# Two-column operations of three norms on GpSimd, and a second variance taken as ScalarE's sum of squares of a Hadamard product

## The reference, cut to what matters

```python
def norm(x):  # over the last axis, eps = 1e-5
    m, v = mean(x), var(x)
    return (x - m) / sqrt(v + eps)

x = x + norm(attention(norm(x), Wq, bq, Wk, bk, Wv, bv, Wo, bo))
xh = norm(x) @ H                     # Hadamard / sqrt(512)
scale = max(max|xh| over the row, 1e-5) / 7
xq = clip(round(xh / scale), -8, 7) * scale
wq = ternary(weight) * scale_w       # one scale for each output row
x = x + norm(xq @ wq.T)
```

## Time and profile before

| | |
|---|---|
| median of three runs | 1216.96 us |
| profiled execution, its own time | 1213.31 us |
| its span | 1211.4 us |
| busy: PE, DVE, ACT, POOL | 91%, 83%, 58%, 49% |

### The profile page before, as it was taken

The page is one execution under the profiler, slowest core; times in us unless marked ns, Lnnn a source line. Parts: engine busy times, 40 slices in busy tenths (PEclk is TensorE's granted clock), DMA queues, the critical chain, the costliest instruction groups (busy, mean ns, idle before and its releaser), DMA issues.

```text
span 1211.4 us, 44874 instructions
## 1 busy us (share of the span) xinstructions
PE 1100.2 (91%) x18625; PEld 726.4 (60%) x18656; DVE 1009.3 (83%) x2558; ACT 702.7 (58%) x1494; POOL 599.1 (49%) x719
## 2 busy tenths in 40 slices
PE   5899999999999999999999999999999999999641
PEld 3566556666666666666566666666666666666320
DVE  5749998888988888899888888988888899887772
ACT  5454566666566566655666665566566655665431
POOL 2333545555454556555545555454556555445422
PEclk9999999999999999999999999999999999999875
DMA  9746665666666576566675656656575566654230
GB/s 271 165 110 138 124 130 136 159 138 136 134 125 137 142 146 153 125 136 138 122 145 137 159 134 137 136 125 132 142 149 145 131 137 138 124 129 102 72 70 36
DMA packets 204687, 161.81 MB, mean 134 GB/s; under 512 B 150432, under 2 KB 150688, under 8 KB 204384
## 3 DMA queue, kind: packets, MB, share of 16 engines
q1 hardware_dynamic: 199600, 141.34, 55.2%
q0 software_dynamic: 4880, 17.57, 4.1%
HBM read 40.87 MB, written 16.78 MB: 48 GB/s over the span
## 4 chain that ended last, share of the span: by engine, by line
PE 56%; DVE 32%; issue 7%; ACT 2%; SPq 1%; DMA 1%; POOL 1%; POOLq 0%; DVEq 0%; ACTq 0%
PE f_job L1281 42%; DVE f_bst L980 6%; PE f_st L1382 3%; DVE f_z L1058 3%; PE f_o L1399 2%; PE f_o L1404 2%; DVE f_o L970 2%; DVE f_inverse L972 2%; PE f_job L1426 2%; DVE f_rmax L948 2%; DVE f_x L1004 2%; DVE f_folded_x L1021 2%; DVE f_y L1012 2%; DVE f_y L1011 2%; DVE f_small L1006 1%
## 5 line engine op out<-in xcount | busy, mean ns | idle before, releaser
L469 POOL TENSOR_SCALAR_AFFINE_SELECT f_PT<-f_PT 64x512 f32<-64x512 f32 (+1 forms) x256 | 202.0, 810 | 68.6 <-ACT f_PT L635 42.8
L484 POOL TENSOR_TENSOR f_square<-f_stage 128x512 bf16<-128x512 f16 x128 | 130.8, 1044 | 130.7 <-ACT f_stage L613 117.5
L1281 PE MATMUL f_job<-f_xTh,f_wqh 128*128 128x256 f16 x512 | 140.8, 275 | 15.6 <-DVE f_wkl L809 14.4
L613 ACT ACTIVATE f_stage<-f_job,f_bias 128x256 f16<-128x256 f32 x256 | 106.0, 465 | 83.7 <-PE f_job L1281 76.9
L475 POOL TENSOR_TENSOR f_OTl<-f_o,f_OTh 128x256 f16<-128x256 f32 x128 | 86.3, 674 | 114.4 <-ACT f_OTh L653 113.6
L1281 PE MATMUL f_job<-f_xTl,f_wqh 128*128 128x256 f16 x512 | 140.2, 274 | 0.0
L1281 PE MATMUL f_job<-f_xTh,f_wql 128*128 128x256 f16 x512 | 140.2, 274 | 0.0
L1281 PE MATMUL f_job<-f_xTh,f_wkh 128*128 128x256 f16 x512 | 139.9, 273 | 0.0
L1281 PE MATMUL f_job<-f_xTh,f_wkl 128*128 128x256 f16 x512 | 139.8, 273 | 0.0
L1281 PE MATMUL f_job<-f_xTl,f_wkh 128*128 128x256 f16 x512 | 139.7, 273 | 0.0
L934 DVE SCALAR_TENSOR_TENSOR f_stage<-f_job,f_bias,f_stage 128x256 f16<-128x256 f32 x256 | 110.7, 474 | 29.5 <-ACT f_stage L613 27.5
(11 more groups left out here) (181 smaller groups left out, 3026.5 us busy)
## 6 DMA issues: line engine op xcount, KB each, us to landing
f_stacks<-f_stage SPq DMA_DIRECT2D x380, 128.0 KB
f_xin<-x SPq DMA_DIRECT2D x32, 512.0 KB, 4.6
f_x<-x SPq DMA_DIRECT2D x32, 512.0 KB, 4.0
out<-f_z POOLq DMA_DIRECT2D x32, 512.0 KB, 3.3
f_Vmix<-f_V SPq DMA_DIRECT2D x32, 256.0 KB, 3.2
f_Vmix<-f_V SPq DMA_DIRECT2D x64, 128.0 KB, 3.4
f_stacks<-rows_const SPq DMA_DIRECT2D x3, 512.0 KB, 7.8
f_stacks<-wqT SPq DMA_DIRECT2D x2, 512.0 KB, 6.0
```

The source lines that it names most:

```text
L469: nc.gpsimd.affine_select(out=d, in_=d, compare_op=ALU.is_ge, fill=0.0, base=odd * SUB, pattern=[[0, 4], [0, TP], [1, SUB]], channel_multi ...
L484: nc.gpsimd.tensor_tensor(square[:, 2 * m + pair, :], h, h, ALU.mult).then_inc(squared, 1)
L613: nc.scalar.activation(stage[:, 2 * m, g, :], bank("qk", g)[:, m * W2:(m + 1) * W2], ACT.Identity, bias=bias[:, m, g:g + 1]).then_inc(qk_h ...
L1281: mm = pe.matmul(dst, lhs[a](c), rhs[b](c), start=(n == 0), stop=(n == 3 * KC - 1))
```

## The change

What it does:

- f, y and z: variance + eps, the negated mean, the products that make the offsets, and z's difference of offsets go from VectorE to GpSimd, next to the powers that were there (`front_columns`, `y_columns`, `z_columns` in the places of the three roots). VectorE only makes `bn_stats` and `bn_aggr`.
- The x norm's statistics go away. ScalarE's new `square_sum` takes the sum of squares of columns 1 to 511 of the Hadamard product (Square with an accumulated output), before `round_levels` of each tile; GpSimd's `z_columns` makes eps from it.
- Column 0 of the quantized levels is a zero that is written once (`q16` gets memory of its own, set to zero at the start); largest magnitude, squares, rounding and levels work on 511 columns.
- ScalarE's order: `square_sum(k-1, 0)` and `round_levels(k-1, 0)` ahead of `front_norm(m, 0)`; `front_norm(m, 1)` behind the first two `exps`.
- The checks of ranges at the end use the new columns, and have one reduction and one addition more.

The diff, cut to its core:

```diff
-        q16 = x2h[:].bitcast(BF16)
+        q16 = sb("q16", [P, TP, D], BF16)
+        unread = sb("unread", [P, TP, D], BF16)
...
+            nc.gpsimd.memset(q16[:], 0.0).then_inc(pool_consts, 1)
+            pool.wait_ge(pool_consts, 7)
...
+            def y_columns(k):
+
+                pool.wait_ge(y_stats_made, TP * k + TP)
+                until(pool, x1_made, TP * k)
+                nc.gpsimd.tensor_scalar(y_veps, y_mv[:, :, 1], EPS, None, ALU.add).then_inc(y_veps_made, 1)
+                nc.gpsimd.tensor_scalar(y_off[:, k, :], y_mv[:, :, 0], -1.0, None, ALU.mult).then_inc(y_turned_sign, 1)
                 pool.wait_ge(y_veps_made, k + 1)
                 nc.gpsimd.tensor_tensor(y_rstd, y_veps, minus_half[:], ALU.pow).then_inc(y_rstd_made, 1)
...
+                pool.wait_ge(y_turned_sign, k + 1)
+                pool.wait_ge(y_rstd_made, k + 1)
+                nc.gpsimd.tensor_tensor(y_off[:, k, :], y_off[:, k, :], y_rstd, ALU.mult).then_inc(y_off_made, 1)
+
+            def z_columns(k):
+
+                pool.wait_ge(qinv_made, TP * k + TP)
+                pool.wait_ge(x_squared, TP * k + TP)
+                nc.gpsimd.tensor_scalar(qeps, x_ss[:, k, :], EPS * (SX * D) ** 2, EPS / D, ALU.add,
+                                        ALU.mult).then_inc(z_step, 1)
+                nc.gpsimd.tensor_tensor(qsquare, qinv, qinv, ALU.mult).then_inc(qsquare_made, 1)
+                pool.wait_ge(z_step, 4 * k + 1)
+                pool.wait_ge(qsquare_made, k + 1)
+                nc.gpsimd.tensor_tensor(qeps, qeps, qsquare, ALU.mult).then_inc(qeps_made, 1)
+                pool.wait_ge(qeps_made, k + 1)
+                pool.wait_ge(z_stats_made, TP * k + TP)
+                nc.gpsimd.tensor_tensor(z_veps, z_mv[:, :, 1], qeps, ALU.add).then_inc(z_step, 1)
+                pool.wait_ge(z_step, 4 * k + 2)
+                until(pool, z_normed, TP * k)
+                nc.gpsimd.tensor_tensor(z_mul, z_veps, minus_half[:], ALU.pow).then_inc(z_step, 1)
+                pool.wait_ge(z_step, 4 * k + 3)
+                nc.gpsimd.tensor_tensor(z_off, z_mv[:, :, 0], z_mul, ALU.mult).then_inc(z_step, 1)
+                pool.wait_ge(z_step, 4 * k + 4)
+                pool.wait_ge(y_off_made, k + 1)
+                nc.gpsimd.tensor_tensor(z_off, y_off[:, k, :], z_off, ALU.subtract).then_inc(z_cols, 1)
...
+            def square_sum(k, t):
+
+                act.wait_ge(qinv_made, TP * k + t + 1)
+                nc.scalar.activation(unread[:, t, 1:D], bank("h", t)[:, 1:D], ACT.Square,
+                                     accum_out=x_ss[:, k, t:t + 1]).then_inc(x_squared, 1)
...
                 qk_high_part(n, 2)
+                if has(k - 1):
+                    square_sum(k - 1, 0)
+                    round_levels(k - 1, 0)
                 if has(m):
                     front_norm(m, 0)
-                if has(k - 1):
-                    round_levels(k - 1, 0)
-                if has(m):
-                    front_norm(m, 1)
...
                 if has(m):
+                    front_norm(m, 1)
                     front_high(m)
                 exps(s, 1, 0)
                 exps(s, 1, 1)
                 if has(k - 1):
+                    square_sum(k - 1, 1)
                     round_levels(k - 1, 1)
...
             def y_stats(k):
                 dve.wait_ge(y_made, TP * k + TP)
-                statistics(0, y, y_mv)
-                nc.vector.tensor_scalar(y_veps, y_mv[:, :, 1], EPS, None, ALU.add).then_inc(y_veps_made, 1)
+                statistics(0, y)
+                until(dve, y_off_made, k)
+                for t in range(TP):
+                    nc.vector.bn_aggr(y_mv[:, t, :], bst[:, 0, t, :]).then_inc(y_stats_made, 1)
...
-                note(nc.vector.scalar_tensor_tensor(y_off[k % 2], y_mv[:, :, 0], -1.0, y_rstd, ALU.mult, ALU.mult))
...
-            def x_stats(k):
-                dve.wait_ge(x1_made, TP * k + TP)
-                for t in range(TP):
-                    note(nc.vector.bn_stats(bst[:, 1, t, :], x1[k % 2][:, t, :]))
-                settled()
-                for t in range(TP):
-                    nc.vector.bn_aggr(x_mv[:, k, t, :], bst[:, 1, t, :]).then_inc(x_stats_made, 1)
...
-                dve.wait_ge(x_stats_made, TP * k + t + 1)
-                sums = bank("h", t)[:, 0:1]
-                note(nc.vector.scalar_tensor_tensor(sums, x_mv[:, k, t, 0:1], -D * SX, sums, ALU.mult, ALU.add))
-                settled()
-                note(nc.vector.tensor_reduce(a, bank("h", t)[:], AX_X, ALU.max, apply_absolute_value=True))
+                note(nc.vector.tensor_reduce(a, bank("h", t)[:, 1:D], AX_X, ALU.max, apply_absolute_value=True))
...
             def z_stats(k):
 
-                dve.wait_ge(qinv_made, TP * k + TP)
-                note(nc.vector.scalar_tensor_tensor(qeps, x_mv[:, k, :, 1], EPS, qinv, ALU.add, ALU.mult))
-                settled()
-                note(nc.vector.scalar_tensor_tensor(qeps, qeps, EPS * (SX / HAD) ** 2, qinv, ALU.mult, ALU.mult))
                 dve.wait_ge(z_made, TP * k + TP)
-                statistics(2, z, z_mv)
-                nc.vector.tensor_tensor(z_veps, z_mv[:, :, 1], qeps, ALU.add).then_inc(z_veps_made, 1)
-
-            def z_columns(k):
-                dve.wait_ge(z_rstd_made, k + 1)
-                note(nc.vector.tensor_tensor(z_off, z_mv[:, :, 0], z_mul, ALU.mult))
-                settled()
-                nc.vector.tensor_tensor(z_off, y_off[k % 2], z_off, ALU.subtract).then_inc(z_cols, 1)
+                statistics(1, z)
+                until(dve, z_cols, k)
+                for t in range(TP):
+                    nc.vector.bn_aggr(z_mv[:, t, :], bst[:, 1, t, :]).then_inc(z_stats_made, 1)
```

More of the change, by code:

```diff
@@ L142, in col @@
             return small[:, n:n + w]
-        f_mv = small[:, 0:4].rearrange("p (t s) -> p t s", s=2)
+        f_mv = sb("f_mv", [P, STEPS, TP, 2], F32)
         f_veps, f_rstd, f_off = col(4), col(6), col(18)
         y_mv = small[:, 8:12].rearrange("p (t s) -> p t s", s=2)
-        y_veps, y_rstd, y_off = col(12), col(14), (col(16), col(20))
-        x_mv = sb("x_mv", [P, STEPS, TP, 2], F32)
+        y_veps, y_rstd = col(12), col(14)
+        y_off = sb("y_off", [P, STEPS, TP], F32)
+        x_ss = sb("x_ss", [P, STEPS, TP], F32)
+        qsquare = col(16)
         z_mv = small[:, 26:30].rearrange("p (t s) -> p t s", s=2)
@@ L243, in fast_path @@
         z_made = sem("z_made")
-        z_veps_made = sem("z_veps_made")
-        z_rstd_made = sem("z_rstd_made")
+        z_stats_made = sem("z_stats_made")
+        qsquare_made = sem("qsquare_made")
+        qeps_made = sem("qeps_made")
+        z_step = sem("z_step")
         z_cols = sem("z_cols")
@@ L446, in _, with front_columns @@
             nc.gpsimd.memset(mh[:, 4 * NH:P], 0.0).then_inc(pool_consts, 1)
-            pool.wait_ge(pool_consts, 6)
+            nc.gpsimd.memset(q16[:], 0.0).then_inc(pool_consts, 1)
+            pool.wait_ge(pool_consts, 7)
             pool.dma_start(bo_bc[:], bo.partition_broadcast(P)).then_inc(bo_in, 16)
-            def front_root(m):
+            def front_columns(m):
+                pool.wait_ge(f_stats_made, TP * m + TP)
+                until(pool, xn_made, TP * m)
+                nc.gpsimd.tensor_scalar(f_veps, f_mv[:, m, :, 1], EPS, None, ALU.add).then_inc(f_veps_made, 1)
+                nc.gpsimd.tensor_scalar(f_off, f_mv[:, m, :, 0], -1.0, None, ALU.mult).then_inc(f_turned_sign, 1)
@@ L518, in _ @@
                 if has(k - 1):
-                    z_root(k - 1)
+                    z_columns(k - 1)
                 if has(s):
@@ L532, in _ @@
             clear_future(last, 1)
-            y_root(last - 1)
+            y_columns(last - 1)
             clear_future(last, 2)
@@ L536, in _ @@
             clear_future(last, 3)
-            z_root(last - 2)
+            z_columns(last - 2)
             heads_low(last, 1)
@@ L541, in _ @@
             finish_out(last - 2)
-            y_root(last)
-            z_root(last - 1)
+            y_columns(last)
+            z_columns(last - 1)
             finish_out(last - 1)
-            z_root(last)
+            z_columns(last)
             finish_out(last)
-            pool.wait_ge(guard_step, 8)
+            pool.wait_ge(guard_step, 9)
             nc.gpsimd.partition_all_reduce(guard2[:], guard[:], P, bass.bass_isa.ReduceOp.max)\
@@ L667, in level @@
                 act.wait_ge(rounded, TP * k + t + 1)
-                nc.scalar.activation(q16[:, t, :], bank("h", t)[:], ACT.Identity, bias=unround_col[:]).then_inc(q_made, 1)
+                until(act, q_turned, TP * (k - 1) + t + 1)
+                nc.scalar.activation(q16[:, t, 1:D], bank("h", t)[:, 1:D], ACT.Identity,
+                                     bias=unround_col[:]).then_inc(q_made, 1)
             def keep_q(k, t):
@@ L759, in _ @@
             exps(last, 0, 0)
+            square_sum(last - 2, 0)
             round_levels(last - 2, 0)
@@ L762, in _ @@
             exps(last, 0, 1)
```

(17 more changed lines are left out.)

75 lines of the change are left out of this document (41 added, 34 removed).

## The result

The changed kernel takes 1219.55 us (median of 16 runs, 1217.23 to 1221.66) against 1216.82 us for the kernel before (16 runs on the same chip, 1214.69 to 1219.40). The ratio of the times is 1.0022, with an interval of 1.0013 to 1.0030. That is 0.2% slower, where 1.5% faster was forecast. The profiled execution has a span of 1215.2 us instead of 1211.4, and its mean granted clock is 0.973 instead of 0.977; from 300 to 900 us it is 1.00 in both.

A forecast was written before the change was run, and what follows sets the result against it. VectorE's 15.2 us stretch from y's second tile to the norms' reduction was taken as on the path in each 35.0 us round. Terms of 0.65, taken as 0.6, times 29 rounds plus 1 in the tail gave 18.4: 1199 us, range 1184 to 1217.

The forecast's parts named there:

- GpSimd's z chain: GpSimd's power plus 7 small operations for z: ends at about the old time and holds nobody up.
- the 19.8 us of the round that I had called free: Rest of the 35.0 us round, belonging to TensorE: VectorE work taken off there wins nothing by itself.
- ScalarE is late: Rival: two square sums don't fit ScalarE's pauses, 0.5 us late each round, 1214; chance 0.14 together with the lock taking all.
- The cover of 0.25 us: ScalarE's pause left before the logarithm after the second square sum uses 0.8 of 1.08 us; any excess delays `normalise`.
- y's variance: y's variance + eps leaving VectorE lets `normalise` start 0.05 us sooner a round, between 0 and 0.13.
- `y_off` and the lock: Line 1006 leaves VectorE; GpSimd's second clearing then blocks `fold`, which wins 0.15 us of 0.54, bounds 0 and 0.54.
- The eps pair of z: Two eps operations of `z_stats` leave VectorE, 592.21 to 592.47: 0.26 us gone a round.
- z's aggregates: VectorE's wait for z's aggregates and variance ahead of `x2_low`: 0.19 us gone a round.
- The price of a small GpSimd operation: Add, sign or product on GpSimd taken as 0.1 us each, so `residual` keeps 0.2 us of cover.
- The rival in which one costs what a power costs: Rival "slower": small GpSimd operations make `residual` 0.95 us late, 1227; decides above 0.5 us each; chance 0.16.
- TensorE's waits: TensorE still waits some 0.7 us for `scale_out`, and has no waits other than its two of now.
- The tail: End of the program, after 1107 us, where VectorE is nearly all of the chain: -1 us, between -3 and +1.

The follow-up runs named there:

- the pair of experiments with the order and the one-column square: Changed kernel with finish_out(k-1) behind heads_low(s, 2) on GpSimd and ScalarE's square sum over one column instead of 511: 1203.94 us, ratio 0.9896 to the kernel before.
- the first experiment: Changed kernel with one edit on GpSimd: finish_out(k-1) behind heads_low(s, 2) instead of ahead of it; 1205.25 us, ratio 0.9898 to the kernel before.

## Why the prediction was wrong

It was wrong in sign: 1199 us was forecast, 1219.55 measured. The range of 1184 to 1217 us lies just below that.

**The step that failed** is the sentence on GpSimd's z chain: it "ends at about the old time, while `norm_z` no longer waits for VectorE to come to its two columns; it holds nobody up." `norm_z` did start sooner, by 1.44 us, though the z chain ends some 0.9 us later in the round than the single power did (596.59 against 595.38, with the stretch 0.32 us later): VectorE's two columns had stood at the end of the norms' reductions. I asked who waits for `norm_z` and found nobody. I did not follow what comes sooner with it: `heads_high(s, 1)` behind it on ScalarE, GpSimd's `heads_low(s, 1)`, and behind that 2.50 us of adds on GpSimd, both operands in SBUF, beside whatever VectorE had there. It had two operations of 0.17 and 0.19 us, which became 0.95 and 1.21. They lie in the 19.8 us of the round that I had called free, and this part got no longer: it is 35.11 - 15.25 = 19.86 us. They did harm through ScalarE, which waits for the `normalise` behind them, makes the scale late, and in the next stretch comes 0.57 us late with the exponential. The page that I had quoted for `y_off` covers both operations: the Trainium skill (SBUF — State Buffer, section Who interferes with whom) counts among those that can contend with GpSimd a `tensor_scalar` that takes both ports for one operand, where its operands allow that (line 1019), besides an instruction with two SBUF inputs (line 1022). The trace agrees, 0.95 against 0.17 us and 1.21 against 0.19; the ports themselves don't show in it. I had applied it to the operations that the change moves, and not to those that it makes meet.

**The rival "ScalarE is late"** names the mechanism of arrival rightly (VectorE idle before `normalise`, no pause before the logarithm) and its cause by half: the square sums measure 0.595 + 0.202 us, as assumed, and fit the pauses by themselves, as the pair of experiments with the order and the one-column square shows. Its condition, that the earlier scale doesn't come, is what happened: `find_scale` was forecast 0.6 us earlier, and ScalarE's first operation behind it starts 7.70 us ahead of the stretch, where it was 7.90 before. Its price of 1214 took 0.5 us of delay off a gain of 0.6; measured are 0.59 of delay and 0.45 of gain. The cover of 0.25 us was not there even without the collision: in the first experiment no pause is left before the logarithm, and the exponential is just in time. The forecast treated the pauses of the earlier trace rows as if they stayed fixed while the change moved what fills them.

**The terms of the 0.65 us a round**, measured in the first experiment, where the collision is gone. Its stretch has 14.75 us instead of 15.20, a gain of 0.45:
- y's variance: `normalise` starts 2.34 us into the stretch instead of 2.41, so 0.07 (forecast 0.05).
- `y_off` and the lock: from `normalise` to `fold` 3.21 us instead of 3.72, so 0.51 won; line 1072 gives 0.47 back beside the second clearing, and line 1080 behind it 0.03. Net 0.01 (forecast 0.15). The mechanism was right, that the lock moves to `fold`; it moved almost whole, which was the lower bound.
- The eps pair of z: 0.14 (forecast 0.26). The statistics start 0.72 us after `scale_out`, where the small operation had started 0.60 after it, so 0.12 of the 0.26 was only the overlap of the follower.
- z's aggregates: 0.17 us to `x2_low` instead of 0.36, so 0.19 as forecast. From `x2_low` to the norms' reduction it is 0.04 less, which the forecast didn't have.

The sum is 0.45 against 0.65, and 29 rounds of it are 13 us, 1.07%, against a measured 1.0%. So without the collision the change gives 1205.25 us: inside the range, and 12.6 us won (the kernel before had 1217.89 on that chip) against 18.4 forecast. In the kernel after, the wait for ScalarE takes all of it: `normalise` starts 0.45 us later instead of 0.07 earlier.

**The price of a small GpSimd operation** was taken as 0.1 us. It is 0.19 to 0.25, with 0.19 to 0.34 from start to start. The line through 256 and 512 columns to 77 ns was no guide to two columns. `residual` has no cover left: in the first experiment the power ends at 582.49, and `residual` starts at 582.53 behind a `normalise` that ends at about the same time. That the three eps operations hardly stretch VectorE was right: in the first experiment lines 1080 and 1081 beside them take 0.45 and 0.42, against 0.42 each before. By the rule that I had quoted, that the later one blocks fully, they would have held it up; the measurement decides. The forecast's "7 small ones" in the z chain are six (lines 490 to 506), besides the power. The rival in which one costs what a power costs is refuted by 0.19 to 0.25 against the 0.5 at which it decided. The estimate by the Trainium skill (GPSIMD Engine Reference, section Performance versus the Vector engine), twice VectorE's time and so 0.32 us (the page measured 2048 columns), is too high by about as much as my 0.1 was too low; the loss it led to did not come, since `residual` wasn't late.

**TensorE's waits.** Forecast 0.7 us for `scale_out`, measured 1.32 in the kernel after and 0.81 in the first experiment; its other wait, for the maxima, is 0.19 instead of 0.56.

**The ends of the program.** Of the 3.8 us of span, up to the first `split_max` the kernel after wins 1.1 us (42.1 instead of 43.3), between the first and the last it loses 2.9, from there to the last tile's Hadamard transform 1.3 (1183.78 instead of 1180.70), and behind it 0.7. The tail was forecast at -1. Its last two parts are about +2. I haven't taken the 1.3 apart. Of the 0.7, 0.6 lies behind the start of the last `norm_z` (19.21 us to the end instead of 18.61), where the range checks have more work. From the transform to that start it is only 0.12 longer: there the two square sums and z's chain of four operations (1.95 us from the aggregates to `norm_z` instead of 1.67) are nearly set off by what went away, as I had assumed.

## What to carry to other kernels

When a change makes an operation start sooner, follow what it releases, and what comes sooner behind it on the same engine, as carefully as who waits for it, and look at what VectorE runs beside it; in these runs a long GpSimd operation did best behind a wait that placed it beside statistics or operations with an operand in PSUM. A pause counted as cover is only cover if the engine still arrives at its old time, and two loads that are each hidden by it can cost together what neither costs alone. And when a locked operation was taken away here, the lock went to the next one: the gain came only when no such operation was left in the place where the other engine's work lay.

## What the runs showed of the hardware

A `TENSOR_SCALAR` of 128x32 on VectorE, with one operand in SBUF (f32 to f16), stood as long beside GpSimd's adds as one with two operands: 0.17 us became 0.95 to 1.12, and 0.19 became 1.21. The first ended at 601.16 and the second at 602.41, some 0.05 us after the adds beside them (599.86 + 1.25 and + 2.50). The change made a third such meeting: the second `x2_low` of a round (line 1086) takes 0.96 us at 598.05 beside `heads_low` (597.80 to 598.46), where it took 0.69 before. It does so in the first experiment too (0.96 at 593.58), and its part in the time was not tested. Statistics over one operand of 128x512 (1.29 us) were not stretched beside a clearing of 1.29 us, and the clearing wasn't either.

On GpSimd, two columns cost 0.22 to 0.25 us as `TENSOR_SCALAR`, 0.19 to 0.20 as `TENSOR_TENSOR` and 0.70 as a power:

```profile
L501 POOL TENSOR_TENSOR f_small<-f_small,f_minus_half 128x2 f32<-128x2 f32 x32 | 22.5, 704 | 2.5
...
L498 POOL TENSOR_TENSOR f_small<-f_small 128x2 f32<-128x2 f32 x32 | 14.3, 446 | 132.1 <-DVE f_small L1115 132.0
...
L503 POOL TENSOR_TENSOR f_small<-f_small 128x2 f32<-128x2 f32 x32 | 6.1, 191 | 2.5
```

They are groups of the kernel after: busy time, mean ns of one, idle time before. Line 498 starts beside `x2_low` and takes 446 ns in the mean, but 0.19 us at 1180.71 in the tail, where VectorE does nothing. z's power comes after it and has 704 ns; before, the power was the one that started beside `x2_low`, and it had a median of 1074.
